# Softmax normalization of the first attention: GpSimd takes three of four probability tiles of heads 0 to 13, VectorE one, ScalarE none

## The chip, the core and the metric

One core of a Trainium2 chip runs the whole program. The metric is the device time of one execution in microseconds; the time of the kernel before is 2398.91 us, the median of three runs (2385.14 to 2401.06). The engines are TensorE (PE, matrix products; PEld is its loading of weights), VectorE (DVE), ScalarE (ACT), GpSimd (POOL), and SyncE (SP), which issues the DMAs. Each runs its own queue in order and waits on semaphores.

## What is computed

A decoder layer on a batch of 8 sequences of 512 tokens and 256 features: self-attention behind a convolution, layer norm, a second attention block (causal and cross), layer norm, a routed feed-forward, layer norm. The change touches the first of these:

```python
q = qkv[:, 0].reshape(b, h, s, hd).astype(jnp.bfloat16)   # h = 16 heads, hd = 16, s = 512
scores = jnp.einsum('bhqd,bhkd->bhqk', q, k) / scale
attn = jax.nn.softmax(scores, axis=-1)                    # in bfloat16
o = jnp.einsum('bhqk,bhkd->bhqd', attn, v)
```

## The kernel before

The eight sequences (called batches, 0 to 7) run one after the other; what ends a batch (its second layer norm and its feed-forward) is woven into the next one, and some of the next batch's projections into this one. Each batch has a stage for the first attention, the projections, and a long stage for the second attention. All orders are written out by hand in five queues, one function per engine.

In the first attention a head has 512 x 512 scores, held as four tiles of 128 rows (NT = 4). For head h:

- TensorE makes the four score tiles in PSUM banks 0 to 3 (L1320), each when VectorE has emptied the same bank of the head before. Behind them in its queue stand the product with V of head h-5 (L1333) and side work: the previous batch's output projection and routing, projections for the next batch, and for heads 8 to 15 the context's keys and values (L1391, L1379), with filler products (L1356) that only keep TensorE running.
- VectorE scales each tile, writes it as bf16 and takes the row minimum (L768).
- ScalarE takes the exponential of each tile and its row sum (L602).
- VectorE takes the reciprocal of the four row sums (L954) when the head's last exponential is done.
- The tiles are multiplied by it, in place in SBUF, bf16. VectorE does three (L961), ScalarE one (L612). In heads 9, 11 and 13 VectorE does all four, and so in heads 14 and 15. ScalarE does its tile of head h-1 behind the exponentials of head h.
- SyncE waits for the head's four tiles and issues one transposing DMA (L410), for heads 0 to 13. Heads 14 and 15 are transposed on TensorE (L1349) and copied by VectorE and ScalarE (L976, L618).
- TensorE multiplies the transposed tiles with V.

Buffers: two heads of scores, five heads of probabilities (E1_SLOTS), two of row sums and reciprocals. VectorE's queue for head h is: reciprocal, tiles, the scores of head h+2 (L768), then side work. For head 2 the side work is the sum L752, which TensorE's projection of the next batch (L1208) needs, and the second layer norm of the previous batch (L782). GpSimd does in this stage only the two small steps of a layer norm's reciprocal root (rstd, L517 and L519); in others it rearranges V (L510) and masks the causal tiles (L528).

Of the kernel before, what the change touches and what calls it, by code (L numbers as in the profile page):

```python
# [37 lines left out]
def decoder_layer(nc, x, xT, ctxT, conv_w, peT, qkT, vT, outT, Wk, bk, Wq, bq, Wv, bv, Wck, bck, Wcq, bcq,  # L38
# [4 lines left out]
    ALU = mybir.AluOpType  # L43
    ACT = mybir.ActivationFunctionType
# [4 lines left out]
    H, HD, P = 16, 16, 128  # L49
    KD = D // P  # L50
    NT = S // P
# [38 lines left out]
    BY_DMA = H - 2  # L90
    ACT_NORMS = [h < BY_DMA and h not in (9, 11, 13) for h in range(H)]
    DVE_TILES = [NT - a for a in ACT_NORMS]
    DVE_PER_BATCH, ACT_PER_BATCH = sum(DVE_TILES), sum(ACT_NORMS)
    PV1_BANKS = (4, 6)
# [20 lines left out]
    with ctx:  # L115
# [3 lines left out]
        def sem(name):  # L119
            return ctx.enter_context(nc.semaphore(name))  # L120
# [128 lines left out]
        qk_ready = sem("qk_ready")  # L249
        rden_ready, p1_dve, p1_act = (sem(n) for n in ("rden_ready", "p1_dve", "p1_act"))  # L250
        p1T_in = [sem(f"p1T_in{i}") for i in range(E1_SLOTS)]
# [19 lines left out]
        def own_wait(engine):  # L271


            engine.sem_inc(waited[engine], 1)
# [117 lines left out]
        def _(sp):  # L392
# [8 lines left out]
            def transpose1(b, h):  # L401

                sp.wait_ge(p1_dve, b * DVE_PER_BATCH + sum(DVE_TILES[:h + 1]))
                own_wait(nc.sync)
                sp.wait_ge(p1_act, b * ACT_PER_BATCH + sum(ACT_NORMS[:h + 1]))
                own_wait(nc.sync)
# [54 lines left out]
        def _(pool):  # L461
            n = [0]
# [58 lines left out]
            def batch(b, prev=True, ahead=True):  # L521
# [8 lines left out]

                if prev:
                    rstd(1, b - 1)
                rstd(0, b)
# [21 lines left out]
        def _(act):  # L555
# [37 lines left out]
            def batch(b, prev=True, ahead=True):  # L593
# [10 lines left out]

                def norm1(h):

                    if h >= BY_DMA:
                        return
                    act.wait_ge(rden_ready, b * H + h + 1)
                    for t in range(DVE_TILES[h], NT):  # L610
                        e = e1[:, h % E1_SLOTS, t, :]
                        nc.scalar.activation(e, e, ACT.Copy, scale=rden1[:, h % 2, t:t + 1]).then_inc(p1_act, 1)  # L612

                def transposed_half(h):
# [46 lines left out]
                for h in range(H):  # L661
                    exp1(h)
                    if h >= 1:
                        norm1(h - 1)
                    if h == 12:
# [68 lines left out]
        def _(dve):  # L734
# [205 lines left out]
            def batch(b, prev=True, ahead=2):  # L940
# [8 lines left out]
                def sum1(h):  # L949

                    dve.wait_ge(e1_ready, (b * H + h + 1) * NT)
                    if h >= 2:
                        dve.wait_ge(p1_act, b * ACT_PER_BATCH + sum(ACT_NORMS[:h - 1]))
                    nc.vector.reciprocal(rden1[:, h % 2, :], den1[:, h % 2, :]).then_inc(rden_ready, 1)  # L954
# [742 lines left out]
```

## Time and profile before

| | |
|---|---|
| median of three runs | 2398.91 us |
| the profiled execution | 2390.6 us |
| its span (first to last instruction) | 2388.9 us |
| mean granted TensorE clock | 0.94 |
| first attention of batch 1 | 325.6 to about 404 us of the span |

The rows are read so: in a timeline, the start in us, the duration in us, engine, line, operation, tiles out<-in, how many are merged, and in brackets how long the engine stood idle before and what ended that. The durations of neighbours overlap a little, so what one costs its queue is the distance of two starts.

### The profile page before, as it was taken

The numbers are of one execution on the slowest core, as the hardware profiler recorded it, in microseconds if no ns is written. First come the engines' busy times: TensorE is split into PE (matmuls) and PEld (weight loads), VectorE is DVE, ScalarE is ACT, GpSimd is POOL, SyncE is SP. The second block draws the span as 40 slices with busy tenths as digits, with TensorE's granted clock in tenths as the row PEclk, the third lists the DMA queues.
The fourth block names the chain that finished last, engine by engine and source line by source line (L and its number), as shares of the span: only waits on it lengthen the run. The fifth ranks groups of instructions, "written<-read, shape, count | busy, mean of one in ns | idle before, by whom it ended". The sixth has DMA issues, their size and how long they took to land.

```text
span 2388.9 us, 37143 instructions
## 1 busy us (share of the span) xinstructions
PE 2205.1 (92%) x12850; PEld 1006.5 (42%) x12866; DVE 1876.4 (79%) x5149; ACT 1406.9 (59%) x2977; POOL 189.1 (8%) x349
## 2 busy tenths in 40 slices
PE   4999989999899998999989998999989999889992
PEld 1345433543345433454335443454334543345432
DVE  5868769788797879888698887988879786878854
ACT  2844678446764578546784466844677456754550
POOL 3011000100011000110001100010001100001000
PEclk8799999999999999999999998999989999789995
DMA  3600025000430006100160002500043000510000
GB/s 102 129 10 1 1 48 95 10 1 1 94 57 10 1 19 112 25 7 1 36 115 10 1 1 55 97 10 1 1 80 62 10 1 10 98 36 1 1 10 9
DMA packets 250843, 81.65 MB, mean 34 GB/s; under 512 B 236064, under 2 KB 247328, under 8 KB 250656
## 3 DMA queue, kind: packets, MB, share of 16 engines
q1 hardware_dynamic: 250656, 79.29, 16.3%
q8 instruction: 102, 1.67, 0.3%
q14 instruction: 85, 0.70, 0.1%
HBM read 16.35 MB, written 4.19 MB: 9 GB/s over the span
## 4 chain that ended last, share of the span: by engine, by line
PE 75%; ACT 11%; DVE 9%; issue 3%; DMA 1%; SPq 0%; POOL 0%; DVEq 0%; POOLq 0%; ACTq 0%
PE bank L1505 22%; PE bank L1558 13%; PE bank L1543 8%; PE bank L1208 7%; ACT work L602 6%; PE bank L1501 5%; PE bank L1460 4%; PE bank L1540 4%; DVE work L768 3%; PE bank L1333 2%; PE bank L1518 2%; ACT o1T L623 2%; PE bank L1320 1%; PE bank L1569 1%; ACT work L658 1%
## 5 line engine op out<-in xcount | busy, mean ns | idle before, releaser
L658 ACT ACTIVATE work<-bank 128x512 f32<-128x512 f32 (+3 forms) x1536 | 737.5, 553 | 561.6 <-PE bank L1543 287.2
L1037 DVE TENSOR_REDUCE top_half<-bank 128x1 f32<-128x512 f32 x1024 | 625.7, 682 | 24.1 <-PE bank L1505 24.1
L1505 PE MATMUL bank<-k_c,q_c 32*128 32x512 f32 x2048 | 630.7, 636 | 0.0
L1543 PE MATMUL bank<-q_c,k_c 32*128 32x512 f32 x2048 | 549.1, 629 | 0.0
L602 ACT ACTIVATE work<-work,neg 128x512 bf16<-128x512 bf16 x512 | 362.8, 718 | 60.7 <-DVE work L768 60.7
L768 DVE TENSOR_SCALAR_CACHE_REDUCE work<-bank 128x512 bf16<-128x512 f32 x512 | 322.4, 687 | 75.4 <-PE bank L1320 43.0
L1505 PEld LDWEIGHTS bank<-k_c,q_c 32*128 32x128 f32 x2048 | 274.5, 185 | 244.5 <-DVE top_half L1037 158.9
L1558 PE MATMUL bank<-work,v_flat 128*32 128x512 f32 (+3 forms) x3072 | 315.3, 545 | 9.2 <-ACT work L658 8.8
L1543 PEld LDWEIGHTS bank<-q_c,k_c 32*128 32x128 f32 x2048 | 227.0, 183 | 92.4 <-ACT work L658 57.2
L1034 DVE CUSTOM_DVE_ANT_0 masked<-bank,mask_w 128x384 bf16<-128x384 f32 (+3 forms) x512 | 223.1, 488 | 53.8 <-PE bank L1501 48.6
L1540 PE MATMUL bank<-q_s,k_s 32*128 32x512 f32 (+3 forms) x1024 | 259.1, 476 | 0.0
L1501 PE MATMUL bank<-k_s,q_s 32*128 32x128 f32 (+3 forms) x1024 | 198.5, 480 | 2.0 <-DVE top_s L1034 1.2
L1558 PEld LDWEIGHTS bank<-work,v_flat 128*32 128x32 f32 x3072 | 91.2, 109 | 234.4 <-issue 130.0
L1320 PE MATMUL bank<-k,q 32*128 32x512 bf16 x448 | 138.1, 401 | 26.6 <-DVE work L768 15.0
L1540 PEld LDWEIGHTS bank<-q_s,k_s 32*128 32x128 f32 x1024 | 141.6, 187 | 23.7 <-issue 8.9
L1333 PE MATMUL bank<-work,v 128*32 128x512 bf16 x512 | 145.2, 413 | 6.1 <-DMA work<-work 5.7
L1501 PEld LDWEIGHTS bank<-k_s,q_s 32*128 32x128 f32 x1024 | 102.9, 186 | 80.6 <-DVE top_s L1034 33.9
L517 POOL TENSOR_SCALAR ln_var<-mv 128x4 f32<-128x4 f32 x32 | 8.7, 272 | 1561.2 <-DVE mv L777 1561.2
L528 POOL TENSOR_SCALAR_AFFINE_SELECT work<-work 128x512 f32<-128x512 f32 x128 | 81.2, 634 | 602.8 <-ACT work L658 602.8
L1049 DVE COPY featA<-bank 128x512 f32<-128x512 f32 x64 | 44.3, 692 | 105.4 <-PE bank L1558 105.4
L961 DVE TENSOR_SCALAR work<-work,rden 128x512 bf16<-128x512 bf16 x424 | 123.0, 350 | 4.5
L602 ACT ACTIVATION_READ_ACCUMULATOR work<-work,neg 128x1 bf16 x512 | 102.3, 200 | 0.0
(191 smaller groups left out, 2260.4 us busy)
## 6 DMA issues: line engine op xcount, KB each, us to landing
xT_pad<-xT SPq DMA_DIRECT2D x16, 256.0 KB, 3.2
ctx_sb<-ctxT SPq DMA_DIRECT2D x8, 512.0 KB, 3.2
x_res<-x SPq DMA_DIRECT2D x8, 512.0 KB, 4.4
out<-r_sb SPq DMA_DIRECT2D x8, 512.0 KB, 3.1
work<-work SPq DMA_TRANSPOSE x112, 4.4
qk_sb<-qkT SPq DMA_DIRECT2D x1, 512.0 KB, 4.7
pe_sb<-peT SPq DMA_DIRECT2D x1, 256.0 KB, 4.4
v_sb<-vT SPq DMA_DIRECT2D x1, 256.0 KB, 5.5
```

What stands on the lines that cost most here:

```text
L602: nc.scalar.activation(e1[:, h % E1_SLOTS, t, :], s1[:, h % 2, t, :], ACT.Exp, bias=neg1[:, h % 2, t:t + 1], scale=-1.0, accum_out=den1[:, ...
L658: nc.scalar.activation(pT[:, s % PT_SLOTS, g, q0:S], exp_bank(n)[:, 0:S - q0], ACT.Exp, scale=SCALE).then_inc(pT_ready, 1)
L768: nc.vector.tensor_scalar(s1[:, h % 2, t, :], bank[:, (NT * h + t) % A1_BANKS, :], -SCALE, None, ALU.mult, ALU.min, accum_out=neg1[:, h % ...
L1034: nc.vector.tensor_tensor_reduce(masked[:, g, 0:n], scores[:, 0:n], mask_w[:, S - n:S], -1.0, -MASKED, ALU.add, ALU.min, top_s[:, i % 2, u ...
L1037: nc.vector.tensor_reduce(top_half[:, i % 2, g, u // 2, u % 2:u % 2 + 1], scores, AX.X, ALU.max, negate=True).then_inc(slot_out, 1)
L1208: last = mm(dst, lhsT(k), rhs(k), start=(k == 0), stop=(k == tiles - 1))
L1333: last = mm(bank[GW * g:GW * (g + 1), PV1_BANKS[h // 8], :], v1[:, h, j, :], p1T[:, h % E1_SLOTS, :, j, :], start=(h % 2 == 0 and j == 0), ...
L1501: mm(dst[:, 0:n], q_s[rows, i, P * u:n], k_s[rows, i, 0:n], start=True, stop=True, tile_position=(GW * g, 0)).then_inc(slot_in, 1)
L1505: mm(dst, q_c[rows, i, P * t:P * (t + 1)], k_c[rows, i, S * half:S * (half + 1)], start=True, stop=True, tile_position=(GW * g, 0)).then_i ...
L1540: mm(dst[:, 0:S - q0], k_s[rows, i, q0:q0 + P], q_s[rows, i, q0:S], start=True, stop=True, tile_position=(GW * g, 0)).then_inc(sT_mm, 1)
L1543: mm(dst, k_c[rows, i, P * u:P * (u + 1)], q_c[rows, i, :], start=True, stop=True, tile_position=(GW * g, 0)).then_inc(sT_mm, 1)
L1558: last = mm(dst[GW * g:GW * (g + 1), q0:S], v_flat[:, at:at + GW], pT[:, s % PT_SLOTS, g, q0:S], start=(s % BURST == 0), stop=(s % BURST = ...
```

## The change

ScalarE's normalization and its semaphore p1_act go. GpSimd gets a function of its own, whose semaphore is p1_pool. VectorE does one tile (t = 0) of heads 0 to 13 and still all four of heads 14 and 15; GpSimd does t = 1 to 3 of heads 0 to 13. SyncE's DMA waits for p1_pool where it waited for p1_act, and so does VectorE's reciprocal, for the tiles of two heads before. GpSimd's rstd(1), the layer norm of the previous batch, stands behind the tiles of heads 0 and 1, and rstd(0) behind those of head 13.

```diff
-    ACT_NORMS = [h < BY_DMA and h not in (9, 11, 13) for h in range(H)]
-    DVE_TILES = [NT - a for a in ACT_NORMS]
-    DVE_PER_BATCH, ACT_PER_BATCH = sum(DVE_TILES), sum(ACT_NORMS)
+    DVE_TILES = [1 if h < BY_DMA else NT for h in range(H)]
+    POOL_TILES = [NT - n for n in DVE_TILES]
+    DVE_PER_BATCH, POOL_PER_BATCH = sum(DVE_TILES), sum(POOL_TILES)
...
-                sp.wait_ge(p1_act, b * ACT_PER_BATCH + sum(ACT_NORMS[:h + 1]))
+                sp.wait_ge(p1_pool, b * POOL_PER_BATCH + sum(POOL_TILES[:h + 1]))
...
-                if prev:
-                    rstd(1, b - 1)
+                def norm1(h):
+
+                    pool.wait_ge(rden_ready, b * H + h + 1)
+                    own_wait(nc.gpsimd)
+                    for t in range(DVE_TILES[h], NT):
+                        e = e1[:, h % E1_SLOTS, t, :]
+                        nc.gpsimd.tensor_scalar(e, e, rden1[:, h % 2, t:t + 1], None, ALU.mult).then_inc(p1_pool, 1)
+
+                for h in range(BY_DMA):
+                    norm1(h)
+                    if prev and h == 1:
+                        rstd(1, b - 1)
...
-                def norm1(h):
-
-                    if h >= BY_DMA:
-                        return
-                    act.wait_ge(rden_ready, b * H + h + 1)
-                    for t in range(DVE_TILES[h], NT):
-                        e = e1[:, h % E1_SLOTS, t, :]
-                        nc.scalar.activation(e, e, ACT.Copy, scale=rden1[:, h % 2, t:t + 1]).then_inc(p1_act, 1)
...
-                    if h >= 1:
-                        norm1(h - 1)
...
-                        dve.wait_ge(p1_act, b * ACT_PER_BATCH + sum(ACT_NORMS[:h - 1]))
+                        dve.wait_ge(p1_pool, b * POOL_PER_BATCH + sum(POOL_TILES[:h - 1]))
```

On ScalarE, in batch 1 from the exponentials of head 8 (L602, L612 in the changed kernel) to those of head 12, before:

```order
L602 ACTIVATE work,den<-work,neg 128x512 x4
L612 ACTIVATE work<-work,rden 128x512
L635 ACTIVATE k_c<-bank,bck_col,live_col 128x512
L602 ACTIVATE work,den<-work,neg 128x512 x4
L612 ACTIVATE work<-work,rden 128x512
L635 ACTIVATE k_c<-bank,bck_col,live_col 128x512
L602 ACTIVATE work,den<-work,neg 128x512 x4
L635 ACTIVATE k_c<-bank,bck_col,live_col 128x512
L602 ACTIVATE work,den<-work,neg 128x512 x4
L612 ACTIVATE work<-work,rden 128x512
L635 ACTIVATE k_c<-bank,bck_col,live_col 128x512
L602 ACTIVATE work,den<-work,neg 128x512 x4
```

and the same place now:

```order
L612 ACTIVATE work,den<-work,neg 128x512 x4
L636 ACTIVATE k_c<-bank,bck_col,live_col 128x512
L612 ACTIVATE work,den<-work,neg 128x512 x4
L636 ACTIVATE k_c<-bank,bck_col,live_col 128x512
L612 ACTIVATE work,den<-work,neg 128x512 x4
L636 ACTIVATE k_c<-bank,bck_col,live_col 128x512
L612 ACTIVATE work,den<-work,neg 128x512 x4
L636 ACTIVATE k_c<-bank,bck_col,live_col 128x512
L612 ACTIVATE work,den<-work,neg 128x512 x4
```

The normalizations (work<-work,rden) are gone and nothing stands in their place; exponentials and copies of the context's keys keep their order.

On GpSimd, from the causal masks of batch 0 (L528) through the first attention of batch 1 to the masks of batch 1, before:

```order
L528 AFFINE_SELECT work<-work 128x4x128 x16
L517 TENSOR_SCALAR ln_var<-mv 128x4
L519 TENSOR_TENSOR ln_r<-ln_var,minus_half 128x4
L517 TENSOR_SCALAR ln_var<-mv 128x4
L519 TENSOR_TENSOR ln_r<-ln_var,minus_half 128x4
L510 COPY v<-v_nat 32x4x4x16 x16
L528 AFFINE_SELECT work<-work 128x4x128 x16
```

and now:

```order
L528 AFFINE_SELECT work<-work 128x4x128 x16
L537 TENSOR_SCALAR work<-work,rden 128x512 x6
L517 TENSOR_SCALAR ln_var<-mv 128x4
L519 TENSOR_TENSOR ln_r<-ln_var,minus_half 128x4
L537 TENSOR_SCALAR work<-work,rden 128x512 x36
L517 TENSOR_SCALAR ln_var<-mv 128x4
L519 TENSOR_TENSOR ln_r<-ln_var,minus_half 128x4
L510 COPY v<-v_nat 32x4x4x16 x16
L528 AFFINE_SELECT work<-work 128x4x128 x16
```

Six tiles (heads 0 and 1) come ahead of rstd(1), and 36 (heads 2 to 13) between it and rstd(0). On VectorE the queue has the same rows, with one tile instead of three or four behind each reciprocal of heads 0 to 13; TensorE's and SyncE's queues are unchanged.

## Rows read from the trace of the kernel before

**Rows 1.** The page: busy us (share of the span) and instructions of each engine.

```profile
PE 2205.1 (92%) x12850; PEld 1006.5 (42%) x12866; DVE 1876.4 (79%) x5149; ACT 1406.9 (59%) x2977; POOL 189.1 (8%) x349
```

**Rows 2.** Stretches: us, busy PE, PEld, DVE, ACT, POOL, then clock, DMA.

```profile
356.12:388.31 32.19, 31.41 (x123) 12.36 (x123) 31.77 (x108) 32.19 (x79) 0.00 (x0) 1.00 0.81 152
67.00:90.00 23.00, 21.37 (x50) 6.18 (x51) 21.39 (x74) 17.74 (x46) 0.00 (x0) 0.68 0.74 148
```

**Rows 3.** Timeline of ScalarE, batch 1: after head 5, and before head 12.

```profile
358.95 0.71 ACT L612 ACTIVATE work<-work,rden 128x512 bf16<-128x512 bf16 x1
359.57 0.71 ACT L602 ACTIVATE work<-work,neg 128x512 bf16<-128x512 bf16 x1
...
382.17 0.78 ACT L635 ACTIVATE k_c<-bank,bck_col,live_col 128x512 f32<-128x512 f32 x1
382.83 0.72 ACT L602 ACTIVATE work<-work,neg 128x512 bf16<-128x512 bf16 x1
```

**Rows 4.** Groups by form: count, busy us, mean ns, idle before and its releaser.

```profile
L612 ACT ACTIVATE work<-work,rden 128x512 bf16<-128x512 bf16 x88 | 62.9, 715 | 19.3 <-DVE rden L954 18.8
...
L768 DVE TENSOR_SCALAR_CACHE_REDUCE work<-bank 128x512 bf16<-128x512 f32 x512 | 322.4, 687 | 75.4 <-PE bank L1320 43.0 <-PE bank L1304 32.4
L961 DVE TENSOR_SCALAR work<-work,rden 128x512 bf16<-128x512 bf16 x424 | 123.0, 350 | 4.5
```

**Rows 5.** Timeline of VectorE, batch 1: head 2, then reciprocals of heads 5, 13, 15.

```profile
346.24 0.18 DVE L954 RECIPROCAL rden<-den 128x4 f32<-128x4 bf16 x1
346.45 0.88 DVE L961 TENSOR_SCALAR work<-work,rden 128x512 bf16<-128x512 bf16 x3
347.25 1.28 DVE L752 TENSOR_TENSOR xs<-bank,xs 128x512 f32<-128x512 f32 x2
...
359.19 0.17 DVE L954 RECIPROCAL rden<-den 128x4 f32<-128x4 bf16 x1
...
391.27 0.18 DVE L954 RECIPROCAL rden<-den 128x4 f32<-128x4 bf16 x1 [1.56 <-ACT work L602]
...
399.05 0.17 DVE L954 RECIPROCAL rden<-den 128x4 f32<-128x4 bf16 x1
```

**Rows 6.** Stretches, ScalarE's normalizations (L612) alone: us, ACT busy (count), clock, DMA.

```profile
356.12:398.70 42.58, 4.99 (x7) 0.96 0.76 142
98.80:119.60 20.80, 1.43 (x2) 0.92 0.69 125
2078.70:2107.40 28.70, 2.14 (x3) 0.88 0.75 124
```

**Rows 7.** Timeline of TensorE, batch 1: behind L752, head 12, the end.

```profile
348.58 3.63 PE L1208 MATMUL bank<-qk_sb,xs 128*128 128x512 f32 x4 [2.87 <-DVE xs L752]
...
377.34 1.03 PE L1320 MATMUL bank<-k,q 32*128 32x512 bf16 x4
...
398.90 1.04 PE L1333 MATMUL bank<-work,v 128*32 128x512 bf16 x4 [0.39 <-DMA work<-work]
400.48 1.05 PE L1349 MATMUL bank<-identb,work 128*128 128x128 bf16 x16 [0.54 <-DVE work L961]
```

**Rows 8.** Groups by form of GpSimd, columns as in rows 4.

```profile
L528 POOL TENSOR_SCALAR_AFFINE_SELECT work<-work 128x512 f32<-128x512 f32 x128 | 81.2, 634 | 602.8 <-ACT work L658 602.8
L510 POOL COPY v<-v_nat 32x256 bf16<-32x256 bf16 x128 | 53.4, 417 | 26.0 <-ACT v_nat L590 17.2 <-POOL ln_r L519 1.8
L519 POOL TENSOR_TENSOR ln_r<-ln_var,minus_half 128x4 f32<-128x4 f32 x32 | 33.8, 1056 | 2.7
L517 POOL TENSOR_SCALAR ln_var<-mv 128x4 f32<-128x4 f32 x32 | 8.7, 272 | 1561.2 <-DVE mv L777 1561.2
```

**Rows 9.** Timeline of GpSimd, batch 1: the first step of rstd(1).

```profile
346.40 0.23 POOL L517 TENSOR_SCALAR ln_var<-mv 128x4 f32<-128x4 f32 x1 [123.73 <-DVE mv L777]
```

**Rows 10.** The transposing DMAs: SyncE's time ns, min/median/max, and issue to landing.

```profile
L410 SPq DMA_TRANSPOSE work<-work x112: 1317/1912/3997, 57.5 to 2101.6; - x112
...
DMA to landing us min/median/max: 4.2/4.4/6.5
```

More of the change, by code:

```diff
@@ L249, in decoder_layer @@
         qk_ready = sem("qk_ready")
-        rden_ready, p1_dve, p1_act = (sem(n) for n in ("rden_ready", "p1_dve", "p1_act"))
+        rden_ready, p1_dve, p1_pool = (sem(n) for n in ("rden_ready", "p1_dve", "p1_pool"))
         p1T_in = [sem(f"p1T_in{i}") for i in range(E1_SLOTS)]
```

## The prediction

> **What bounds the kernel now.** I read the page's busy times first, then the groups of instructions by form, then the stretches and the timelines of the first attention in batch 1. GpSimd is busy 8% of the span [rows 1]; VectorE 79%, ScalarE 59%, TensorE 92%. Those are averages, and the change lives in one stage only: the first attention. There ScalarE is full. From the exponentials of head 5 to those of head 13 (356.12 to 388.31) ScalarE is busy 32.19 of 32.19 us, VectorE 31.77, TensorE 31.41 [rows 2]. So three engines run level and GpSimd stands still. The reader is to see that the gain of unloading one of them ends where the next one stands.
>
> What sets the pace there is ScalarE: four exponentials and one normalization per head, back to back. Its normalization of head 4 starts at 358.95 and the exponentials of head 6 at 359.57, so one tile takes 0.61 to 0.62 us of its queue [rows 3]; by form it is 88 tiles at 715 ns, and neighbours overlap by 0.1 [rows 4]. VectorE waits 1.56 us for ScalarE ahead of head 13's reciprocal [rows 5], which says the same from the other side.
>
> **The change, part by part.**
> Tiles: 448 tiles of heads 0 to 13 are normalized in all 8 batches. Before, ScalarE does 88, and VectorE 360 (its 424 [rows 4] less the 64 of heads 14 and 15). After, VectorE does 112 and GpSimd 336.
>
> (a) ScalarE loses 88 tiles. Of the 11 in a batch, 7 lie in the full stretch 356.12 to 398.70, 2 in that of batch 0 and 3 in that of batch 7 [rows 6]. The others stand where ScalarE waits for TensorE's dense matrix products anyway, and save nothing. In batches 1 to 6: 7 x 0.61 = 4.3 us. Batch 0: 1.2. Batch 7: 1.8.
>
> (b) VectorE loses two tiles of most heads, three of heads 9, 11 and 13. One tile takes (0.88 - 0.35)/2 = 0.27 us of its queue [rows 4, 5]. This lies on the path at one place: head 2's three tiles stand ahead of the sum L752, which TensorE waits 2.87 us for [rows 5, 7]; 2 x 0.27 = 0.53 us earlier, and with it all that follows, second layer norm included. In batch 0 two heads, where VectorE is the slower one, give 1.1 instead; batch 7 0.5, since its next scores hang on the same queue. Elsewhere VectorE's saving only keeps it out of the way: between the reciprocals of heads 5 and 13 it works 391.27 - 359.19 - 1.56 = 30.5 us and loses 18 tiles, 4.8 us, so 25.7, against ScalarE's 32.2 - 6 x 0.61 = 28.5.
>
> (c) TensorE keeps its work, and it is the next limit. Head 12's score products start at 377.34 [rows 7]; 0.5 earlier by (b), with 0.3 for the first product, 0.7 for VectorE's pass and 0.15 of waits, ScalarE can begin head 12 at 378.0. ScalarE wants it at 382.83 - 3.66 - 0.53 = 378.6 [rows 3]. The cover is 0.6 us at its thinnest. After that the 2.3 us copy of o1T on ScalarE gives TensorE its lead back.
>
> (d) GpSimd gains 336 tensor_scalars, 128x512 bf16 in place with a column of factors. The trace has none. Nearest is its 128x512 affine_select, 634 ns; the same opcode on 4 elements takes 272; copies of 256 bf16 elements take 417, which by the element would be 0.83 us for 512; the far end is the power of 4 elements, 1056 ns [rows 8]. Below, VectorE's 0.35 us; a faster GpSimd than that buys nothing, as it is hidden. I take 0.65, by the affine_select, which has the same elements per lane. A head then costs GpSimd 3 x 0.65 = 1.95 us, plus 0.16 (it starts 0.16 us after VectorE's own next instruction [rows 5, 9]) and up to 0.35 behind VectorE's tile: 2.5 us a head against the 2.9 to 3.5 that the others take.
>
> (e) Waits. VectorE's reciprocal of head h now waits for GpSimd's head h-2; behind it stand its tile and the scores of h+2, for which ScalarE waits. At 2.5 us that wait was over a head ago. The transposing DMA of a head waited for VectorE and ScalarE, and ScalarE did its tile only behind the next head's exponentials; now most heads are ready earlier. Heads 9, 11 and 13, which VectorE did alone, are ready about 1.3 us later. That matters for head 13 only. With T its reciprocal (391.27): 0.18 + 0.16 + 0.35 + 1.95 + 0.15 to the issue, 4.4 to land [rows 10], 1.0 for the products with V: T + 8.2. TensorE also waits for head 15: its reciprocal at 399.05 is T + 7.8, the transposition at 400.48 T + 9.2 [rows 5, 7]. With the normalizations gone, heads 14 and 15 take ScalarE 2 x (4 x 0.71 + 0.66) = 7.0 (the copies of k_c take 0.66 each [rows 3]), then 1.35 for reciprocal and four tiles: T + 8.4. So head 13 hides by 0.2 us, and it pays from 0.72 us a tile on. GpSimd's rstd(1) stands behind head 1's tiles and still waits for its input, so it starts at 346.40 as before [rows 9] and holds head 2's tiles back by 1.3 us, with heads to spare.
>
> Sum: batches 1 to 6: 6 x (4.3 + 0.5) = 28.8; batch 0: 1.2 + 1.1 = 2.3, batch 7: 1.8 + 0.5 = 2.3; together 33.4. I take off 1.4 for head 13's transfer, which lands in 4.2 to 6.5 us [rows 10]: **32 us less**. The profiled execution took 2390.6, which gives 2358.6. It lies 8.3 below the median of the runs shown, 2398.91, so I forecast 2367 for the median.
>
> **A rule against it.** VectorE does a 512-element bf16 tile in 350 ns and an fp32 pass of as many in 690 [rows 4], so its normalization runs in a fast mode. The Trainium skill (SBUF — State Buffer, Who interferes with whom) says that a VectorE instruction in a 2-port mode and a GpSimd instruction exclude each other, and the later one fully blocks. No row here shows the two together. By that rule the order decides, and the second rival below is what it would make of the time if GpSimd came first.
>
> **Rivals.**
> 1. TensorE paces. For: 31.41 of 32.19 us busy [rows 2], a cover of 0.6 us. Then a batch gains the idle 0.8 plus 0.5: 8 x 1.2 = about 10 us, 2389. Against: part of that busy time is filler products (L1356), and it is ahead of need everywhere but at head 12.
> 2. GpSimd's tile stands in VectorE's way. If each VectorE tile waits 0.63 us for one of GpSimd's, VectorE needs 25.7 + 8 x 0.63 = 30.7 us for what ScalarE does in 28.5; a batch gains 4.8 - 2.2 = 2.6 us and all eight about 18: 2381. Against: VectorE starts 0.16 us before GpSimd [rows 5, 9], and at 2.5 us a head GpSimd is done before the next tile.
> 3. GpSimd takes 0.9 to 1.1 us a tile. Head 13 is 0.5 to 1.1 us late, and at 1.1 a head costs 3 x 1.1 + 0.5 = 3.8 us against ScalarE's new mean of (39.9 - 4.3)/10 = 3.55, so 9 x 0.25 = 2.2 more: 1.5 to 4.3 us a batch are left, about 20 in all at the middle, 2379. The copies' 0.83 by the element speaks for its edge, the affine_select against it.
> 4. The other side: GpSimd paces. A head takes (399.05 - 359.19)/10 = 3.99 us now, side work included. GpSimd with 3t + 0.5 passes that at t = 1.16 us a tile. At 1.25 it would be 4.25 a head, 9 x 0.26 = 2.4, and head 13 is ready 0.8 us past T + 9.2: 3.2 us more a batch, 8 x 3.2 = 26, 2425. For: the power's 1056 ns for 4 elements shows that its instructions can be dear. Against: its plain 512-element pass is 634.
> 5. More: TensorE had a mean granted clock of 0.68 from 67 to 90 us [rows 2], that is 2 x 0.32 x 23 = 15 us at 1.2 GHz instead of 2.4, after waits for VectorE. If shorter waits keep the full level there, half of that, some 7 us, comes on top: 2360 or less with the other batches' share.
>
> **How the numbers follow.** The forecast 0.53 (its own range 2355 to 2375); rival 1 0.12; 2 0.11; 3 0.07; 4 0.11; 5 0.06. The range 2350 to 2392 leaves out rival 4, and the far ends of 1 and 5, together under 0.2. One per cent, 24 us, is about what can be told from no change. Faster by more holds for the forecast and rival 5 and a little of 3: 0.60. Rival 4 less its mild cases is slower: 0.09. The rest, 0.31, is the same.
>
> **What would show it.** ScalarE's line of normalizations gone, 336 on GpSimd at about 650 ns. In batch 1, reciprocal 5 to reciprocal 13 in 28.4 us instead of 32.1, TensorE's start behind L752 0.5 earlier, each middle batch 4.8 us shorter. GpSimd's line with a wait for the reciprocal, and none of VectorE's reciprocal for GpSimd. Wrong if VectorE's single tile shows more than 0.35 us or starts late (rival 2), if TensorE shows no idle at all to 388 (rival 1), if VectorE's reciprocals wait for GpSimd (4), or if TensorE waits for the last DMA over 0.5 us (3).

## The result, and the profile after

| | before | after |
|---|---|---|
| median | 2397.15 us (4 runs) | 2468.67 us (4 runs) |
| span of the profiled execution | 2388.9 us | 2465.9 us |
| mean granted TensorE clock | 0.940 | 0.927 |

The changed kernel is slower: ratio 1.0311, 95% interval 1.0275 to 1.0346, some 75 us. The forecast was 32 us less. Each later kernel is compared with runs of the kernel before that were taken beside it, so the time before differs a little from one to the next (2390.64 to 2393.74 us).

The page of the kernel after, its busy line and the shares of the chain of waits that ended last, then three of its costliest groups (busy us, mean ns, idle before and its releaser):

```profile
PE 2227.9 (90%) x12866; PEld 1022.7 (41%) x12866; DVE 1846.0 (75%) x4901; ACT 1356.2 (55%) x2889; POOL 709.2 (29%) x685
...
PE 69%; POOL 14%; DVE 7%; issue 5%; ACT 3%; DMA 2%; SPq 0%; DVEq 0%; POOLq 0%; ACTq 0%
...
L537 POOL TENSOR_SCALAR work<-work,rden 128x512 bf16<-128x512 bf16 x336 | 520.2, 1566 | 249.5 <-DVE rden L953 249.5
...
L612 ACT ACTIVATE work<-work,neg 128x512 bf16<-128x512 bf16 x512 | 362.1, 712 | 90.9 <-DVE work L767 90.7
```

Against [rows 1], ScalarE lost 51 us of work and VectorE 30, as meant, and GpSimd gained 520. One number says why the time went up: a GpSimd tile takes **1566 ns**, where the prediction took 650. GpSimd is 29% busy over the whole span, yet it is 14% of the chain that ended last. The timeline of GpSimd in batch 1 shows how (start, duration, engine, line, operation, tiles, how many, idle before):

```profile
347.90 0.23 POOL L517 TENSOR_SCALAR ln_var<-mv 128x4 f32<-128x4 f32 x1 [5.77 <-DVE mv L776]
348.21 1.04 POOL L519 TENSOR_TENSOR ln_r<-ln_var,minus_half 128x4 f32<-128x4 f32 x1
349.26 4.73 POOL L537 TENSOR_SCALAR work<-work,rden 128x512 bf16<-128x512 bf16 x3
354.55 50.95 POOL L537 TENSOR_SCALAR work<-work,rden 128x512 bf16<-128x512 bf16 x33 [0.56 <-DVE rden L953]
```

From head 3 to head 13 it runs 33 tiles in 50.95 us without a gap: 1.54 us a tile, 4.62 a head. VectorE's timeline of the same stretch holds the waits that follow, the ones that the prediction named as the sign of its fourth rival:

```profile
364.02 0.18 DVE L953 RECIPROCAL rden<-den 128x4 f32<-128x4 bf16 x1 [0.61 <-POOL work L537]
...
368.64 0.18 DVE L953 RECIPROCAL rden<-den 128x4 f32<-128x4 bf16 x1 [1.14 <-POOL work L537]
...
400.95 0.18 DVE L953 RECIPROCAL rden<-den 128x4 f32<-128x4 bf16 x1 [0.87 <-POOL work L537]
401.17 2.32 DVE L960 TENSOR_SCALAR work<-work,rden 128x512 bf16<-128x512 bf16 x4
...
408.27 0.69 DVE L975 COPY work<-bank 128x1024 bf16<-128x1024 bf16 x1 [2.83 <-PE bank L1348]
408.87 0.17 DVE L953 RECIPROCAL rden<-den 128x4 f32<-128x4 bf16 x1
```

Reciprocals 6 and 7 are 4.62 us apart, three tiles, and each waits for GpSimd's tiles of two heads before. Three stretches, from reciprocal 5 to reciprocal 13, at the stage's end, and far behind it (us, busy PE, PEld, DVE, ACT, POOL, granted clock, DMA share, GB/s), of the kernel after:

```profile
360.20:396.30 36.10, 30.20 (x111) 10.74 (x111) 27.10 (x86) 32.03 (x81) 36.10 (x25) 1.00 0.73 132
404.00:409.00 5.00, 3.70 (x20) 2.06 (x20) 2.04 (x6) 0.00 (x0) 1.50 (x1) 0.50 0.68 134
440.90:455.90 15.00, 15.00 (x58) 8.17 (x59) 9.73 (x42) 2.93 (x5) 0.00 (x0) 0.77 0.00 1
```

The full engine is now GpSimd, 36.10 of 36.10, where it was ScalarE [rows 2]. TensorE at the stage's end, after:

```profile
400.76 1.58 PE L1332 MATMUL bank<-work,v 128*32 128x512 bf16 x4 [2.60 <-DMA work<-work]
405.30 1.89 PE L1332 MATMUL bank<-work,v 128*32 128x512 bf16 x4 [2.96 <-DMA work<-work]
407.12 1.89 PE L1348 MATMUL bank<-identb,work 128*128 128x128 bf16 x16
410.01 1.89 PE L1332 MATMUL bank<-work,v 128*32 128x512 bf16 x4 [1.00 <-DMA work<-work]
```

In the order of TensorE's queue these are the products with V of heads 11 and 12, the transposition of head 14, and the products of head 13. [rows 7] has the last of them with a wait of 0.39 us. Products of the same shape take 1.89 us instead of 1.04: the granted clock is 0.50 from 404 to 409 us, the half level (1.2 GHz). The chain at the end reads: GpSimd's tiles of head 12, their DMA, the products of head 12 that wait 2.96 us, the transposition of head 14 behind them, VectorE's copy that waits 2.83 us for that, and only then reciprocal 15. The products of head 13 come later than reciprocal 15.

The 77 us between the two spans can be laid out batch by batch, from the starts of the reciprocals. "Stages" runs from head 0's to head 15's, summed over eight batches; "rests" is from there to the next batch's head 0, summed over seven. "Clock" is the part of the rests that TensorE's lower clock accounts for: (1 - granted clock) times the length, added up over stretches of about 5 us, good to about 1 us. "5 to 13" and "13 to 15" are what most of the batches 1 to 6 show. Later experiments are put into the same table:

| kernel | stages | rests | clock in the rests | 5 to 13 | 13 to 15 | span |
|---|---|---|---|---|---|---|
| before | 546.5 | 1505.7 | 25 | 32.1 | 7.8 | 2388.9 |
| after | +55.3 | +21.3 | +17 | 36.1 | 12.5 | +77.0 |
| p1_d3 | +6.7 | +9.7 | +14 | 33.1 | 7.9 | +15.9 |
| p2_d2 | -20.6 | +10.0 | +10 | 31.1 | 7.7 | -10.9 |
| p2_fill | -6.5 | +8.9 | +9 | 31.1 or 34.7 | 7.7 | +4.8 |
| half | -39.4 | +28.6 | +32 | 29.6 | 7.0 | -8.1 |
| half_fill | -34.4 | +16.1 | +17 | 29.6 | 7.0 | -17.6 |
| t0 | -35.4 | +10.5 | +9 | 29.6 | 7.0 | -24.2 |
| tt3 | -31.8 | +30.0 | +29 | 29.6 | 7.0 | -1.6 |
| tt3_fill | -31.7 | +6.7 | +2 | 29.6 | 7.0 | -24.0 |
| tt_last | -34.4 | -0.2 | +2 | 29.6 | 8.3 | -38.7 |
| tt_last_fill | -21.9 | +2.2 | +7 | 29.6 | 8.3 | -20.2 |
| before_fill | -6.1 | +10.9 | +14 | 32.1 | 7.8 | +4.4 |

(What is missing to the span lies ahead of the first reciprocal and behind the last.) Each row is one execution. That of tt_last is 10 us quicker than its median and that of p2_fill 14 us slower than its own, and single batches with a lower clock stand in several (see the last section), so the row and the median can differ. Two terms are to be explained: the stages, and the rests, in which the change touches no instruction. The fourth column answers for most of the rests: it follows the third within 5 us in every row.

### The profile page after: what moved, and what is told of

Read it like the earlier page. It is cut to its first block, busy times and chain, and to the rows that moved or that the text cites. A ratio compares the mean times of both kernels' runs of the same rounds, so it can differ in the third digit from the quotient of the medians.

```text
span 2465.9 us, 37247 instructions
## 1 busy us (share of the span) xinstructions
PE 2227.9 (90%) x12866; PEld 1022.7 (41%) x12866; DVE 1846.0 (75%) x4901; ACT 1356.2 (55%) x2889; POOL 709.2 (29%) x685
## 4 chain that ended last, share of the span: by engine, by line
PE 69%; POOL 14%; DVE 7%; issue 5%; ACT 3%; DMA 2%; SPq 0%; DVEq 0%; POOLq 0%; ACTq 0%
PE bank L1504 21%; POOL work L537 14%; PE bank L1557 13%; PE bank L1542 8%; PE bank L1207 6%; PE bank L1500 5%; PE bank L1459 4%; PE bank L1539 4%; DVE work L767 2%; DMA work<-work 1%; PE bank L1517 1%; PE bank L1568 1%; PE bank L1332 1%; ACT work L659 1%; PE bank L1298 1%
## 5 line engine op out<-in xcount | busy, mean ns | idle before, releaser
L537 POOL TENSOR_SCALAR work<-work,rden 128x512 bf16<-128x512 bf16 x336 | 520.2, 1566 | 249.5 <-DVE rden L953 249.5
L612 ACT ACTIVATE work<-work,neg 128x512 bf16<-128x512 bf16 x512 | 362.1, 712 | 90.9 <-DVE work L767 90.7
L528 POOL TENSOR_SCALAR_AFFINE_SELECT work<-work 128x512 f32<-128x512 f32 x128 | 81.2, 634 | 608.3 <-ACT work L659 608.3
L1332 PE MATMUL bank<-work,v 128*32 128x512 bf16 x512 | 153.5, 431 | 80.6 <-DMA work<-work 80.4
L1332 PEld LDWEIGHTS bank<-work,v 128*32 128x32 bf16 x512 | 42.6, 102 | 174.0 <-DMA work<-work 113.6
```

What stands on the lines that cost most here:

```text
L537: nc.gpsimd.tensor_scalar(e, e, rden1[:, h % 2, t:t + 1], None, ALU.mult).then_inc(p1_pool, 1)
L612: nc.scalar.activation(e1[:, h % E1_SLOTS, t, :], s1[:, h % 2, t, :], ACT.Exp, bias=neg1[:, h % 2, t:t + 1], scale=-1.0, accum_out=den1[:, ...
L1332: last = mm(bank[GW * g:GW * (g + 1), PV1_BANKS[h // 8], :], v1[:, h, j, :], p1T[:, h % E1_SLOTS, :, j, :], start=(h % 2 == 0 and j == 0), ...
```

## The experiments

The expectations speak of three theories. A: GpSimd's own price of a tile sets the pace. B: GpSimd and VectorE slow each other. C: a late head 13 leaves TensorE idle, and what it then runs at a lower clock is lost behind the stage. S, or S', is the sum of the forecast without such a loss, or with another cause for it.

### forms: what GpSimd charges when it is alone

The kernel before, with twenty GpSimd instructions in its setup, in front of the first batch.

```diff
+            for _ in range(2):
+                init(nc.gpsimd.tensor_scalar(f_e, f_e, col, None, ALU.mult))
+                init(nc.gpsimd.tensor_scalar(f_e[:, 0:256], f_e[:, 0:256], col, None, ALU.mult))
+                init(nc.gpsimd.tensor_scalar(f_e, f_e, 1.0, None, ALU.mult))
+                init(nc.gpsimd.tensor_scalar(f_o, f_e, col, None, ALU.mult))
+                init(nc.gpsimd.tensor_scalar(g_e, g_e, col, None, ALU.mult))
+                init(nc.gpsimd.tensor_scalar(g_e, g_e, 1.0, None, ALU.mult))
+                init(nc.gpsimd.tensor_copy(f_o, f_e))
+                init(nc.gpsimd.tensor_copy(g_o, g_e))
+                init(nc.gpsimd.tensor_tensor(g_e, g_e, col.broadcast_to([P, S]), ALU.mult))
+                init(nc.gpsimd.tensor_tensor(f_e, f_e, f_o, ALU.mult))
```

> The kernel before with twenty GpSimd instructions of 128 partitions put into its setup, each waited for, while VectorE and ScalarE do nothing beside them. It prices the disputed tile by form. Changed kernel: 1.55 us for a 128x512 bf16 tensor_scalar with a column of factors. Theory A (the form is dear in itself): the same form takes 1.5 to 1.6 us here too, its half of 256 elements about 0.8 to 0.9. Theory B (the price is contention with VectorE, which runs beside it in the changed kernel): 0.6 to 0.8 us here. Within A: if the column of factors is what costs, the same multiplication by a constant takes 0.6 to 0.7; if bf16 is, the fp32 forms take 0.6 to 0.7; if the general multiply loop is, all of them take about 1.5 and only the plain copy 0.6. The setup gets some 20 us longer, so the whole time says nothing.

The timeline of GpSimd in this kernel, first pass of the loop:

```profile
16.72 1.58 POOL L508 TENSOR_SCALAR work<-work,rden 128x512 bf16<-128x512 bf16 x1
18.40 0.92 POOL L509 TENSOR_SCALAR work<-work,rden 128x256 bf16<-128x256 bf16 x1
19.41 1.49 POOL L510 TENSOR_SCALAR work<-work 128x512 bf16<-128x512 bf16 x1
20.99 1.56 POOL L511 TENSOR_SCALAR work<-work,rden 128x512 bf16<-128x512 bf16 x1
22.64 1.56 POOL L512 TENSOR_SCALAR work<-work,rden 128x512 f32<-128x512 f32 x1
24.29 1.49 POOL L513 TENSOR_SCALAR work<-work 128x512 f32<-128x512 f32 x1
25.84 0.61 POOL L514 COPY work<-work 128x512 bf16<-128x512 bf16 x1
26.52 0.61 POOL L515 COPY work<-work 128x512 f32<-128x512 f32 x1
27.21 1.04 POOL L516 TENSOR_TENSOR work<-work,rden 128x512 f32<-128x512 f32 x1
28.33 1.16 POOL L517 TENSOR_TENSOR work<-work 128x512 bf16<-128x512 bf16 x1
```

With no attention running beside it, the tile costs 1.56 us. So the price is the form's own. It is not contention, nor the element type (fp32 the same), nor being in place (L511 writes elsewhere), and the column of factors is 0.07 of it (L510 has a constant). 256 columns take 0.92, so a column costs (1.56 - 0.92)/256 = 2.5 ns and the start 0.28 us. The same product written as tensor_tensor, with the factor's column spread over the row, costs a third less: 1.04 (L516). A plain copy takes 0.61, close to the affine_select of [rows 8] on which the prediction leaned: at one number of elements the opcode makes the price.

### p1_d3 and p2_d2: fewer tiles on GpSimd

```diff
-    DVE_TILES = [1 if h < BY_DMA else NT for h in range(H)]
+    DVE_TILES = [3 if h < BY_DMA else NT for h in range(H)]
```

and the same with 2 for p2_d2.

> GpSimd one tile, VectorE three, of heads 0 to 13; ScalarE none. Theory A (the forecast's structure holds and only the tile's price was wrong): GpSimd needs 1.56 + 0.5 us a head and hides. ScalarE would need 28.5 us from the reciprocal of head 5 to that of head 13, VectorE 30.5 less two tiles of 0.27, so 30.0, and sets the pace: 32.1 becomes about 30.1, and with head 13's one tile less some 2.3 us a batch, 15 to 20 us faster than before, about 2380. Theory B (GpSimd beside VectorE costs VectorE 0.2 us for each tile and more for the layer norm, so that any share for GpSimd is a loss): three tiles at +0.2 eat 0.6 a head, the stretch takes 32 to 35 us and the time is that of before or up to 10 us above.

> GpSimd two tiles, VectorE two, of heads 0 to 13; ScalarE none. Theory A: GpSimd needs 3.1 + 0.2 us a head, just below the 3.5 to 4.0 of a head, and VectorE 28 us for the stretch from reciprocal 5 to reciprocal 13 (30.5 less 10 tiles of 0.27), ScalarE 28.5: the stretch takes about 29, head 13 is ready at 9.0 us behind its reciprocal instead of 9.2 before; about 3 us a batch, 20 to 28 us faster than before. Theory B: VectorE's two tiles at +0.2 and waits for the reciprocals of two heads before: same as before or slower.

p1_d3: 2404.39 us (9 runs) against 2390.64 (24 runs), ratio 1.0057 (1.0039 to 1.0074). p2_d2: 2381.42 (10 runs), ratio 0.9958 (0.9934 to 0.9983). VectorE and GpSimd in batch 2, of p1_d3:

```profile
641.94 1.31 DVE L960 TENSOR_SCALAR work<-work,rden 128x512 bf16<-128x512 bf16 x3
...
642.11 1.61 POOL L537 TENSOR_SCALAR work<-work,rden 128x512 bf16<-128x512 bf16 x1 [2.27 <-DVE rden L953]
```

and of p2_d2:

```profile
638.24 1.05 DVE L960 TENSOR_SCALAR work<-work,rden 128x512 bf16<-128x512 bf16 x2
...
638.41 3.16 POOL L537 TENSOR_SCALAR work<-work,rden 128x512 bf16<-128x512 bf16 x2 [0.46 <-DVE rden L953]
```

With one tile GpSimd idles 2.3 to 2.9 us ahead of every head, so A alone would have let p1_d3 gain. It lost about 14 us. In the stages the reason is B: VectorE's three tiles take 1.31 us instead of 0.88 [rows 5] while GpSimd's runs beside them, and VectorE sets the pace. From reciprocal 5 to 13 of batch 2, p1_d3:

```profile
641.74:674.89 33.15, 29.95 (x103) 10.37 (x102) 32.87 (x103) 29.47 (x74) 12.92 (x8) 1.00 0.69 128
```

VectorE is busy 32.87 of 33.15 us. The 30.0 us of the expectation and 8 heads at 0.43 us more make 33.4. That explains the stages (+6.7 us in the table) only; the other 9.7 us lie in the rests, with the clock. In p2_d2 VectorE's pair takes 1.05 instead of 0.62, again 0.43 more, but with a tile less to do. Of its shortest heads, 3.62 us, GpSimd's two tiles fill 3.16: they are hidden. There too it is VectorE that paces, busy 30.77 of 31.05 us from reciprocal 5 to 13 of batch 2, and so the gain was 10 us and not the 20 to 28 of theory A.

### half and t0: GpSimd's tile made cheaper

GpSimd does 256 of the tile's 512 columns, or 4 of them; the rest stay unnormalized, all else is as in the changed kernel.

```diff
-                        e = e1[:, h % E1_SLOTS, t, :]
+                        e = e1[:, h % E1_SLOTS, t, 0:S // 2]
```

(t0 has `0:4` there.)

> The changed kernel, but GpSimd multiplies only the first 256 of 512 columns in each of its three tiles (the other half of the keys of these tiles stays without its factor, so this part of the computation is left out). It halves GpSimd's price and leaves all queues and waits as they are. Theory A: a tile takes 0.8 to 0.9 us, a head 3 x 0.85 + 0.5 = 3.0 us, which hides; head 13 lands 0.4 us late a batch; the sum of the forecast then gives 28 to 31 us less than before, 2366 to 2369. Theory B: VectorE is held up wherever GpSimd runs, and most of the gain is missing: 0 to 10 us less than before.

> The changed kernel with GpSimd multiplying 4 of 512 columns in each of its three tiles (the rest of these tiles stays without its factor, so that part of the computation is left out): all queues and waits of the change, at 0.28 us a tile. It says what the change could bring if GpSimd were free. Theory S (the forecast's sum holds where GpSimd is not late): 33 us less than before. Theory C (TensorE's waits at the end of the stage make the granted clock fall some 30 us later, which the sum left out; with a tile of 0.9 us that took back 4 to 5 us a batch): head 13 is not late here, so TensorE waits only for VectorE's last tiles, and the fall stays as before; 25 to 33 us less, and the stretch from 30 to 45 us behind the stage at a mean clock near 0.89. If that stretch is at 0.8 or less though no DMA is late, the shorter stage itself shifts the clock, and only 5 to 15 us are gained.

half: 2383.27 us (10 runs) against 2390.64, ratio 0.9966 (0.9941 to 0.9991). t0: 2365.61 (4 runs) against 2392.25 (18 runs), ratio 0.9883 (0.9868 to 0.9898), 28 us less. GpSimd's line in half and in t0 (duration ns min/median/max):

```profile
L537 POOL TENSOR_SCALAR work<-work,rden x336: 912/921/979, 53.6 to 2089.8; 128x256 bf16<-128x256 bf16 x168
```

```profile
L537 POOL TENSOR_SCALAR work<-work,rden x336: 284/290/353, 55.3 to 2076.3; 128x4 bf16<-128x4 bf16 x168
```

t0 is the change as the prediction meant it, with a GpSimd that costs next to nothing. It gains 28 us where the sum had 33, so steps (a) to (c) hold in their total. A tile of 0.92 us is hidden just as well inside the stage: both have 29.6 and 7.0 us. Yet half is 20 us slower than t0, and the table puts that outside the stages: its rests are 29 us longer than before's, 4 us a batch. The 8 us that half gained are what theory B had forecast for it, but B isn't the reason: VectorE's tiles keep their 353 ns in half as in t0 (356 at most). TensorE's timeline in batch 2 of half:

```profile
670.26 1.22 PE L1348 MATMUL bank<-identb,work 128*128 128x128 bf16 x16
673.74 1.24 PE L1332 MATMUL bank<-work,v 128*32 128x512 bf16 x4 [2.27 <-DMA work<-work]
674.91 1.89 PE L1348 MATMUL bank<-identb,work 128*128 128x128 bf16 x16
```

Here is the prediction's third rival: TensorE waits 2.27 us for head 13's DMA. Little of that wait is lost directly. It ends behind reciprocal 15 (673.10), so it doesn't show in 13 to 15, and the transposition of head 15 behind it, which waits for VectorE's tiles in any case, starts 1.8 to 2.5 us behind reciprocal 15, in t0 1.6. Most of what is lost is lost by the clock, in two places. One is right behind the wait. The first 5 us behind reciprocal 15, in batch 2 of half:

```profile
673.10:678.10 5.00, 4.36 (x27) 2.85 (x28) 3.36 (x12) 2.48 (x3) 0.00 (x0) 0.66 0.01 2
```

In half this is 0.66, or 0.50 in batches 0 and 7; before had 1.00 in all eight. With the 5 us behind it, it makes 14 of the 32 us in the clock column. The other place is further on: 32 to 47 us behind reciprocal 15 half has a granted clock of 0.77 in seven batches, 0.79 in the last, where before had 0.89 in five. In t0, where no DMA is late, it is 0.89 in two batches only, and 0.66 to 0.82 in six, so that second dip is not head 13's alone.

### half_fill, p2_fill and before_fill: filler products in the gap

Filler products (the kernel's own keep_clock) where TensorE would wait at the stage's end: four at head 15, eight ahead of head 13's products with V. The kernel before got six.

```diff
+                    if h == 15:
+                        pe.wait_ge(o1_copied, b * KD + 1)
+                        keep_clock(4, 4)
...
                 transpose_tiles(H - 2)
+                keep_clock(4, 8)
                 pv1(H - 3)
```

> Run half (GpSimd 256 of 512 columns of its tiles, 0.92 us each) with twelve filler products on TensorE in the last part of the stage, where it waits: four ahead of the last context-key product, eight ahead of head 13's product with V. Nothing waits for them. Theory C (clock): the idle of 2.3 us for head 13's DMA is filled, the stretch behind comes back from a mean clock of 0.77 to about 0.89, half's gain of 8 us grows to 20 to 30. Theory S' (the later loss has another cause, such as the late heads themselves): no change to half within 4 us, or some us slower by the fillers' own 0.24 us each.

> GpSimd two tiles, VectorE two (run p2_d2), with the same twelve filler products. p2_d2 had 2.5 us of waits for the DMAs of heads 12 and 13 and a mean clock of 0.66 in the stretch 30 to 45 us behind the stage. Theory C: the clock comes back to about 0.89, which gives 3.4 us a batch, so 25 to 30 us in place of the 10 that p2_d2 gained. Theory S': as p2_d2, within 4 us.

> The kernel before with six filler products in the same places (four ahead of the last context-key product, where TensorE waits 1.4 us, two ahead of head 13's product). It has no GpSimd tiles and tests the clock by itself. Theory C: the mean clock behind the stage rises above 0.89 in most batches, 3 to 10 us less. Rival (the clock behind the stage does not hang on the idle at its end): no change within 3 us, or 3 to 5 us slower by the fillers.

half_fill: 2371.10 us (4 runs), ratio 0.9897 (0.9865 to 0.9928), while half had 0.9966: by the ratios the fillers bring some 16 us, by the medians 12, and they take 12 off the rests. p2_fill: 2381.45 (10 runs), 0.9969 (0.9940 to 0.9999), no different from p2_d2. before_fill: 2390.79 (12 runs) against 2393.74 (17 runs), 0.9996 (0.9973 to 1.0020): nothing. The first 5 us behind reciprocal 15, in batch 2 of half_fill:

```profile
671.33:676.33 5.00, 4.49 (x35) 2.40 (x34) 3.97 (x14) 2.48 (x3) 0.00 (x0) 1.00 0.03 5
```

Stretches far behind the stage, of half:

```profile
705.10:720.10 15.00, 15.00 (x53) 7.43 (x53) 9.65 (x44) 3.10 (x5) 0.00 (x0) 0.77 0.01 2
```

and of half_fill, at the same distance:

```profile
703.33:718.33 15.00, 15.00 (x64) 7.58 (x62) 10.41 (x45) 5.62 (x7) 0.00 (x0) 0.89 0.01 2
```

TensorE is busy 15.00 of 15.00 us in both; at a clock of 0.89 it gets through 64 instructions, at 0.77 through 53.

The first part of C is shown: the clock falls right behind the long wait (2.0 to 2.6 us) in all eight batches of half and, with the fillers in it, in none. The second part is not. Half_fill's batches are mixed further on, 0.89 in two of them and 0.66 or 0.67 in four. And p2_fill speaks against it: p2_d2's longest waits are 1.3 to 1.8 us, and the fillers cut TensorE's idle time between reciprocal 13 and 3 us behind reciprocal 15 from 2.6 to 0.2 us in most batches, yet 32 to 47 us behind reciprocal 15 the clock stays at 0.66 to 0.79 in all eight, and the time is that of p2_d2, where C had said 25 to 30 us less than before. So that dip has a cause which no run here isolates. Nor is the length of one wait the whole of the first part. In before_fill TensorE waits 1.7 to 2.3 us for a DMA in every batch, and the clock stays at 1.00 from reciprocal 13 to 5 us behind reciprocal 15; t0 falls to 0.66 in the first 5 us behind reciprocal 15 in two batches, with no wait over 1.8 us. The sum of the waits is no guide either: TensorE idles 4.2 us at the stage's end in most batches of t0 and 3.4 in half.

### tt3: the same work in GpSimd's cheaper form

```diff
-                        nc.gpsimd.tensor_scalar(e, e, rden1[:, h % 2, t:t + 1], None, ALU.mult).then_inc(p1_pool, 1)
+                        nc.gpsimd.tensor_tensor(e, e, rden1[:, h % 2, t:t + 1].broadcast_to([P, S]), ALU.mult).then_inc(p1_pool, 1)
```

> The changed kernel with another form of GpSimd's instruction for the same result: tensor_tensor with the column of factors broadcast along the row, 1.04 us for 512 fp32 elements in run forms, where tensor_scalar took 1.56. A tile at 1.05 to 1.15 us makes a head 3 x 1.1 + 0.5 = 3.8 us against 3.55 on average for ScalarE. Theory S alone (the forecast's structure): 10 to 15 us less than before. With theory C, 1.1 us of waiting for head 13 and a lower clock behind the stage take 3 to 4 us a batch on top: 10 to 20 us more than before, some 55 to 65 less than the changed kernel.

2387.81 us (9 runs) against 2392.25, ratio 0.9979 (0.9963 to 0.9995). GpSimd's line of tt3, and VectorE's:

```profile
L537 POOL TENSOR_TENSOR work<-work,rden x336: 1031/1035/1107, 54.5 to 2100.1; 128x512 bf16<-128x512 bf16 x168
```

```profile
L960 DVE TENSOR_SCALAR work<-work,rden x176: 347/353/476, 54.4 to 2105.6; 128x512 bf16<-128x512 bf16 x176
```

Nothing but the opcode differs from the changed kernel, and 80 us are gone. That settles A for the stages: 5 to 13 falls from 36.1 to 29.6 us, as with half and t0. VectorE's single tile keeps its 353 ns in the median. What is left is the clock again: TensorE waits 2.33 to 2.60 us for head 13, the clock right behind reciprocal 15 is 0.51 or 0.66 in seven of eight batches, and the rests are 30 us longer than before's, which eats nearly all of the 32 us that the stages gained.

### tt_last, tt3_fill and tt_last_fill: head 13 in time, or its gap filled

Two cures for the same gap. tt_last gives VectorE three of head 13's tiles, so that its DMA starts earlier:

```diff
-    DVE_TILES = [1 if h < BY_DMA else NT for h in range(H)]
+    DVE_TILES = [1 if h < BY_DMA - 1 else 3 if h < BY_DMA else NT for h in range(H)]
```

tt3_fill is tt3 with the twelve filler products shown above, tt_last_fill is tt_last with eight.

> Run tt3 (GpSimd three tiles by tensor_tensor, 1.04 us each) with head 13 alone divided the other way: VectorE three of its tiles, GpSimd one. Head 13 is ready 2.1 us earlier and VectorE's queue 0.5 us longer there. Theory C (late head 13 makes TensorE wait 2.3 us at the end of the stage, and the clock falls behind it): the wait for that DMA goes to 0.3 or less, what lies between the reciprocal of head 15 and the next batch's first goes from 220 to 217, stage 63.6 instead of 63.1: some 2.5 us a batch, 20 to 25 us less than before, where tt3 had 5 less. If the loss behind the stage is not from head 13: 5 to 10 less than before, as tt3.

> tt3 with twelve filler products in the places of half_fill. The waits for head 13 stay; only TensorE's idle is filled. Theory C: as half to half_fill (16 us): from 5 less to about 20 less than before. Rival: the late head itself costs, and nothing comes back: within 4 us of tt3.

> tt_last with eight filler products on TensorE in the last part of the stage (four ahead of the last context-key product, where it waits 1.1 us for ScalarE, four ahead of head 13's product with V). Theory C: the clock behind the stage comes up once more, 25 to 32 us less than before, the quickest of all. Rival: what idle is left is too little to matter, and the fillers do nothing or cost 1 us a batch: 15 to 25 less.

Against 2393.74 us (17 runs): tt_last 2361.97 (6 runs), ratio 0.9869 (0.9841 to 0.9897), about 31 us less. tt3_fill 2361.85 (4 runs), 0.9868 (0.9835 to 0.9901). tt_last_fill 2368.44 (6 runs), 0.9885 (0.9855 to 0.9915). TensorE at the end of batch 2's stage, of tt_last:

```profile
663.38 1.04 PE L1332 MATMUL bank<-work,v 128*32 128x512 bf16 x4 [0.99 <-DMA work<-work]
...
668.72 1.06 PE L1348 MATMUL bank<-identb,work 128*128 128x128 bf16 x16 [1.43 <-DVE work L960]
```

Those are the products of head 12 and the transposition of head 15. Head 13's products, between them, no longer wait. TensorE idles there no less than in tt3 (3.8 us against 3.6 in most batches), but in shorter pieces, none above 1.5 us, and the clock right behind reciprocal 15 is 1.00 in all eight batches. The rests are back to those of before (-0.2 us in the table). The price is 1.3 us a stage. VectorE's two extra tiles are 0.53 of it; the other 0.78 is theory B, GpSimd's tile beside VectorE's (shown at rival 2 below). The gain of 31 us is more than the 20 to 25 expected, and the six executions of tt_last lie within 15 us.

Filling the gap does as much: in tt3_fill the clock right behind reciprocal 15 is 1.00 in all batches and the rests are down from +30.0 to +6.7 us. Both together do no more than either; tt_last_fill was expected to be the quickest and wasn't. tt_last and tt3_fill keep the whole computation and are quicker than both kernels; between them no difference was measured.

## Why the prediction was wrong, step by step

**(d) failed, and it alone turned the sign.** It read "GpSimd gains 336 tensor_scalars" and took 0.65 us for each "by the affine_select, which has the same elements per lane". Measured: 1.566 us in place, 1.56 alone. The term was mis-sized 2.4 times, and even its stated bounds, 0.35 to 1.056, didn't hold the value. The nearest row by opcode was in [rows 8], 272 ns on 4 elements, and t0 shows that this was right (290 ns): it is the start-up. The slope, 2.5 ns a column, could not be read from any row. With the tile at 290 ns (t0) the kernel gains 28 us, at 1.566 us it loses 75, and all else is the same. The copies' 417 ns for 256 elements point to 0.83 for a copy, and a plain copy is 0.61. What was wrong is to take a slope from another opcode and call the span of such rows a bound.

**Rival 4 happened.** "GpSimd with 3t + 0.5 passes that at t = 1.16 us a tile" names the right mechanism. With the measured t it would give 5.2 us a head; measured were 4.62, since the 0.5 falls away once the queue never runs dry. The rival stopped at t = 1.25 and 2425 us. At 1.54 its own steps give 9 x (4.62 - 3.99) = 5.7 us a batch ahead of reciprocal 15, and the stage of batch 1 grew by 9.3: 4.0 between reciprocals 5 and 13, 4.8 between 13 and 15, 0.5 ahead of them. The part that was too small is the end. Step (e) said of a late head that it "matters for head 13 only". In the changed kernel it is head 12: its products wait 2.96 us, and they stand ahead of the transposition of head 14, whose copy stands ahead of reciprocal 15. Another 21 us lie in the rests, 17 of them by the clock, and no step or rival had them.

**(a), (b), (c), the pace of ScalarE, held in the sum and not part by part.** "28.4 us instead of 32.1" between reciprocals 5 and 13: 29.6 with t0, half and tt3, so 2.5 of the 3.7 us. The 1.2 us missing are seen in t0, in the stretch from reciprocal 5 to 13 of batch 1 (columns as above) and in ScalarE's timeline in it:

```profile
351.47:381.08 29.61, 29.21 (x110) 10.52 (x109) 25.83 (x85) 28.72 (x73) 7.09 (x24) 1.00 0.88 167
```

```profile
361.25 0.78 ACT L636 ACTIVATE k_c<-bank,bck_col,live_col 128x512 f32<-128x512 f32 x1 [0.70 <-PE bank L1390]
```

ScalarE's own work is 28.72 us, near the 28.5 of step (b). It waits 0.90 us for TensorE's context keys (0.70 and once 0.20), and TensorE is busy 29.21 of 29.61. So rival 1, a TensorE that paces, is there as well, for 0.9 us a batch; step (c) looked for it at head 12 alone, and it stands at the copies of k_c. The 7.0 us that "heads 14 and 15 take ScalarE" held as well: from reciprocal 13 to 15 ScalarE is busy 6.99 of 6.99 us in t0. The first five heads gained more than the 0.5 us of (b), 0.7 in batch 1 and 1.3 to 2.4 in batches 2 to 6, and the stages of batches 0 and 7 are 6.7 and 4.9 us shorter where the sum had 2.3 each. The stages are 35 us shorter in t0, against 33 in the sum, in spite of one batch of the slow kind, and the rests take 10 back. That 28 comes so near to 33 is in part luck.

**(e) left out the clock.** Of head 13's transfer it said "it pays from 0.72 us a tile on". At 0.92 and at 1.035 us TensorE waits over 2 us for head 13. Of this the transposition of head 15 loses 0.2 to 0.9 us a batch in half and 0.9 to 1.5 in tt3 (0.3 in its last batch), against t0, near the 0.5 to 1.1 of rival 3; in half_fill, where the products run at the full level, it starts as in t0. But the wait was priced inside the stage only. Behind the stage it goes with 4 us a batch (half +28.6, tt3 +30.0 in the rests), and that is why tt3 measures 5 us less than before where rival 3, which covers its 1.035 us, said 20. Some 2 us of the 4 come right behind the wait and go when it is filled; for the others the cause is open.

**Rival 2, the two engines in each other's way,** is true in part, though not by the size it gave. In the changed kernel VectorE's tile is on average 481 ns, the four tiles of head 14 take 2.32 us instead of 1.14, and the second layer norm slows too (kernel before, then after):

```profile
350.88 1.38 DVE L782 TENSOR_SCALAR r_sb<-x_res,mv,ln_r 128x256 f32<-128x256 f32 x4
```

```profile
351.85 2.28 DVE L781 TENSOR_SCALAR r_sb<-x_res,mv,ln_r 128x256 f32<-128x256 f32 x4
```

There it is not what sets the pace: VectorE works 27.10 of 36.10 us. In p1_d3 it is. The rule that the prediction cites, the Trainium skill (SBUF — State Buffer, Who interferes with whom), has the later instruction fully blocked. Tile by tile the traces agree in one form and not in the other. In p1_d3 and tt_last the first of VectorE's three tiles starts ahead of GpSimd's and takes 0.35 us. The second starts behind it. In p1_d3, with GpSimd's tensor_scalar from 642.11 to 643.72 (above), the second tile is

```profile
642.21 0.78 DVE L960 TENSOR_SCALAR work<-work,rden 128x512 bf16<-128x512 bf16 x1
```

It loses 0.43 us and is over at 642.99, 0.73 us ahead of GpSimd's end: not fully blocked. In tt_last, beside tensor_tensor in head 13 of batch 2 (GpSimd, then VectorE):

```profile
659.97 1.11 POOL L537 TENSOR_TENSOR work<-work,rden 128x512 bf16<-128x512 bf16 x1 [1.81 <-DVE rden L953]
660.09 1.13 DVE L960 TENSOR_SCALAR work<-work,rden 128x512 bf16<-128x512 bf16 x1
```

Here the second tile loses 0.78 us and ends at 661.22, 0.14 us behind GpSimd's (661.08), in all eight batches alike: as by the rule. So the form of GpSimd's instruction decides how much VectorE loses. GpSimd's ends are rough in a profile, and why the two forms differ, no run here tells.

**Rival 5, a clock gain,** went the other way: 0.927 after instead of 0.940. With the tile made cheap, t0, it was 0.946.

## What to carry to other kernels

An operation that a trace does not show had no bound here from other opcodes on the same engine: on GpSimd the same 512 columns cost 0.61, 1.04 or 1.56 us by the form of the instruction alone. Before moving a pass to an idle engine, time that exact form in the setup of the kernel, where ten forms took 13 us. And price a late transfer also by what TensorE does after it: in half and tt3 a wait of over 2 us ahead of a dense phase went with 4 us more in that phase, and filling the wait gave 12 and 23 of the 29 and 30 us back, breaking it up all 30. In the kernels with shorter waits the fillers gave nothing.

## What the runs showed of the hardware

GpSimd's tensor_scalar is slower than its tensor_tensor for the same product, 1.56 against 1.04 us, although the second names two tensors; neither element type nor an output elsewhere matters to the first. Against that, a VectorE tile that starts behind GpSimd's tensor_tensor is held to its end (1.13 us instead of 0.35), behind its tensor_scalar only 0.43 us longer.

The same stage of one kernel runs at two paces. In t0, batch 3 takes from reciprocal 5 to 13:

```profile
915.73:950.72 34.99, 34.59 (x119) 12.77 (x118) 25.91 (x87) 28.31 (x71) 7.04 (x24) 0.87 0.79 148
```

With a granted clock of 0.87 instead of the 1.00 of batch 1 (shown above) the stretch takes 5.4 us more: TensorE is busy 34.59 us of it and has no slack there. In six of the thirteen profiled executions laid out above, one to three of the batches 1 to 6 are of the slow kind, so one profile of a kernel may stand well off its median: p2_fill's, with three of them, was 2395.39 at a median of 2381.45. Which batch is slow isn't explained here.
